# Output product of the mixture's rounds in two banks of its own and in three pieces, GpSimd's root ahead of its sums

## The reference, cut to what matters

```python
x = x + _L0_attn_ref(_layernorm(x), ...)            # ends with: out @ Wo + bo
x = x + _L0_xattn_ref(_layernorm(x), ctx_1024, ...) # out @ Wo + bo
x = x + _L0_ffn_ref(_layernorm(x), ...)
# in _L0_ffn_ref, up to the routing
rms = jnp.mean(xf * xf, axis=-1, keepdims=True)
normed = (xf * jax.lax.rsqrt(rms + EPS) * norm_weight).astype(jnp.bfloat16)
logits = (einsum('bsh,eh->bse', nf, gate_weight) + gate_bias)
scores, idx = jax.lax.top_k(logits, K)              # K = 2 of 8 experts
w = jax.nn.softmax(scores, axis=-1)
```

## Time and profile before

| what | us |
|---|---|
| runs: lowest, median, highest of 3 | 2040.12, 2045.48, 2047.65 |
| the profiled execution | 2038.56 |
| its span (first to last instruction) | 2036.8 |
| TensorE, VectorE, ScalarE, GpSimd busy in the span | 1861.0, 1299.9, 975.3, 970.7 |
| mean granted TensorE clock | 0.963 of full speed |

### The profile page before, as it was taken

How to read it: one execution, slowest core, us unless ns; L and a number is a source line. 1 busy time by engine, 2 the same in 40 slices (tenths; PEclk the granted TensorE clock), 3 DMA queues, 4 the chain that set the end, 5 groups by cost and what they waited for, 6 DMA issues and landing times.

```text
span 2036.8 us, 52538 instructions
## 1 busy us (share of the span) xinstructions
PE 1861.0 (91%) x21476; PEld 1544.5 (76%) x21476; DVE 1299.9 (64%) x2932; ACT 975.3 (48%) x1984; POOL 970.7 (48%) x783
## 2 busy tenths in 40 slices
PE   7999999999999999987649579999999999988994
PEld 5677777777777777766437479999899999987883
DVE  6667676767676766647756665456556554556983
ACT  3666666666666666532235233334443343344551
POOL 2555555555555555545633743344234333435441
PEclk9999999999999999999879789999999999999997
DMA  6101020101230100225134520000221000220000
GB/s 243 55 19 47 19 78 19 51 19 71 102 130 20 50 9 12 73 101 164 45 120 130 157 93 13 18 18 13 80 80 28 19 19 18 69 84 22 12 17 16
DMA packets 74606, 119.85 MB, mean 59 GB/s; under 512 B 8392, under 2 KB 64464, under 8 KB 70992
## 3 DMA queue, kind: packets, MB, share of 16 engines
q1 hardware_dynamic: 69392, 105.31, 15.4%
q0 software_dynamic: 2560, 6.30, 1.1%
q10 hardware_dynamic: 2416, 4.88, 0.7%
HBM read 76.61 MB, written 39.85 MB: 57 GB/s over the span
## 4 chain that ended last, share of the span: by engine, by line
PE 37%; POOL 5%; DVE 4%; DMA 3%; issue 3%; ACT 2%; SPq 1%; POOLq 0%; DVEq 0%; ACTq 0%
PE psum L265 12%; PE psum L276 8%; PE psum L2036 3%; PE psum L2024 2%; PE psum L2534 2%; PE psum L2010 1%; POOL b_yg L1487 1%; PE psum L225 1%; PE psum L2568 1%; POOL xs L1477 1%; PE psum L246 1%; PE psum L1352 1%; PE psum L1369 1%; ACT e_pr L2673 1%; DMA b_x_in<-in_x 1%
## 5 line engine op out<-in xcount | busy, mean ns | idle before, releaser
L774 POOL TENSOR_TENSOR a_sm<-a_sm,a_rsum 128x1024 f32<-128x1024 f32 x256 | 480.1, 1895 | 355.6 <-DVE a_rsum L808 353.2
L796 DVE CUSTOM_DVE_ANT_0 a_sm<-psum,a_strip 128x1024 f32<-128x1024 f32 x256 | 312.0, 1219 | 145.3 <-PE psum L628 145.3
L709 ACT ACTIVATE a_sm<-a_sm,a_mn 128x1024 f32<-128x1024 f32 x256 | 293.9, 1148 | 28.2 <-DVE a_mn L796 27.1
L714 ACT ACTIVATE a_pT<-psum 128x512 f32<-128x512 f32 x256 | 151.6, 592 | 272.4 <-PE psum L641 272.4
L641 PE MATMUL psum<-ident,a_sm 128*128 128x128 f32 x2048 | 275.2, 277 | 5.7 <-POOL a_sm L774 4.6
L641 PEld LDWEIGHTS psum<-ident,a_sm 128*128 128x128 f32 x2048 | 223.8, 140 | 62.9 <-issue 46.0
L656 PE MATMUL psum<-a_pT,a_V 128*64 128x256 f32 x2048 | 249.0, 385 | 0.6 <-ACT a_o L720 0.6
L656 PEld LDWEIGHTS psum<-a_pT,a_V 128*64 128x64 f32 x2048 | 136.1, 136 | 77.3 <-issue 22.1
L803 DVE COPY a_pT<-psum 128x512 f32<-128x512 f32 x256 | 174.9, 683 | 12.6 <-PE psum L641 5.4
L2120 ACT ACTIVATE g_val<-psum 128x512 f32<-128x512 f32 x64 | 38.0, 597 | 215.8 <-PE psum L2036 215.6
L628 PE MATMUL psum<-a_KH,a_QH 64*128 64x512 f32 x512 | 114.3, 443 | 2.5 <-DVE a_mn L796 2.5
(11 more groups left out here) (396 smaller groups left out, 3764.9 us busy)
## 6 DMA issues: line engine op xcount, KB each, us to landing
a_strip<-table SPq DMA_DIRECT2D x16, 960.0 KB, 6.7
oT<-a_o SPq DMA_DIRECT2D x64, 128.0 KB, 1.9
xs<-b_zeros SPq DMA_DIRECT2D x8, 1024.0 KB, 4.1
b_oT_in<-oT SPq DMA_DIRECT2D x7, 1024.0 KB, 5.7
y<-b_yb SPq DMA_DIRECT2D x23, 256.0 KB, 2.2
b_xs<-xs SPq DMA_DIRECT2D x23, 128.0 KB, 2.2
a_raw<-in_a_wqkv SPq DMA_DIRECT2D x7, 384.0 KB, 3.4
s_x<-in_x_rev SPq DMA_DIRECT2D x4, 512.0 KB, 8.2
```

The lines of the kernel that those rows point to most:

```text
L709: a.activation(sm[:, st % RING, :], sm[:, st % RING, :], ACT.Exp, scale=-1.0, bias=mn[:, at:at + 1], accum_out=rsum[:, at:at + 1]).then_in ...
L714: a.activation(probs(st, 0), psum[:, 4, :].rearrange("p (k q) -> p k q", k=4), ACT.Copy).then_inc(sig("pT_act"), 1)
L774: g.tensor_tensor(sm[:, st % RING, :], sm[:, st % RING, :], rsum[:, at:at + 1].broadcast_to([P, T]), ALU.mult).then_inc(sig("scaled"), 1)
L796: v.tensor_tensor_reduce(out=sm[:, st % RING, :], in0=scores_banks(hl).rearrange("p c n -> p (c n)"), in1=strip[:, pair % 2, hl, qt * P:qt ...
```

## The change

On TensorE the product `ay` gets two banks for itself and the other stages six. Its 16 steps are now three pieces: 2 steps (`ay_0`) behind `mT`, 6 (`ay_1`) behind `bs`, 8 (`ay_2`) behind `mr`. On GpSimd the root "mn" stands ahead of `first_sum`, and the sum of x1 last. The conversion of `w2` on ScalarE is made in two halves, in rounds 4 and 6, and whoever waited for two signals of `wide` waits for three.

```diff
-        every = [("ay", a + 1), ("mT", c), ("mg", c), ("bT", a), ("bp", b), ("by", b), ("bs", a), ("mr", c), ("ay_rest", a + 1)]
-        if r == 0:
-            every = [("ay", 1), ("ay_rest", 1)]
+        every = [("mT", c), ("ay_0", a + 1), ("mg", c), ("bT", a), ("bp", b), ("by", b), ("bs", a), ("ay_1", a + 1),
+                 ("mr", c), ("ay_2", a + 1)]
...
-            if stage != "ay_rest":
-                turns.add(sig, [(stage, s)], range(8))
+            if stage == "ay_0":
+                turns.add(sig, [("ay", s)], range(2))
+            elif stage[:2] != "ay":
+                turns.add(sig, [(stage, s)], range(2, 8))
...
-        sp.wait_ge(sig("wide"), 2)
+        sp.wait_ge(sig("wide"), 3)
...
-        def attended(s, t):
+        def attended(s, part):
             bank = banks("ay", s)
...
+            for i in range(*((0, 2), (2, HP), (HP, PT * HP))[part]):
+                t, k = i // HP, i % HP
...
+            if part == 2:
+                last.then_inc(sig("ay_ps"), 1)
...
-            if r == 4:
+            if r in (4, 6):
                 a.wait_ge(have("w2b"), 16)
-                a.activation(w2[:, :, :, :], w2b[:, :, :, :], ACT.Copy).then_inc(sig("wide"), 1)
+                some = slice(0, E0 // 2) if r == 4 else slice(E0 // 2, E0)
+                a.activation(w2[:, some, :, :], w2b[:, some, :, :], ACT.Copy).then_inc(sig("wide"), 1)
...
+            if b < NP:
+                norm_rstd(g, sig, "mn", b, mn, mhalf)
             if s + 1 < NP:
                 first_sum(s + 1)
-            if s < NP:
-                g.wait_ge(sig("bn_h"), PT * (s + 1))
-                g.tensor_tensor(x1[s % 2][:, :, :], x1[s % 2][:, :, :], over_tiles(bo_b[:, :], PT), ALU.add).then_inc(sig("x1_bo"), 1)
             if b < NP:
-                norm_rstd(g, sig, "mn", b, mn, mhalf)
                 g.wait_ge(sig("m_ss"), PT * (b + 1))
...
+            if s < NP:
+                g.wait_ge(sig("bn_h"), PT * (s + 1))
+                g.tensor_tensor(x1[s % 2][:, :, :], x1[s % 2][:, :, :], over_tiles(bo_b[:, :], PT), ALU.add).then_inc(sig("x1_bo"), 1)
```

More of the change, by code:

```diff
@@ L1258, in tensor @@
     def tensor(pe, then):
-        def attended(s, t):
+        def attended(s, part):
             bank = banks("ay", s)
[L1261 to L1264, removed]
+            for i in range(*((0, 2), (2, HP), (HP, PT * HP))[part]):
+                t, k = i // HP, i % HP
+                last = pe.matmul(bank[:, t * D:(t + 1) * D], (early["next"] if s == 1 else slots[s % 3])[0][:, k, t * P:(t + 1) * P],
+                                 wo[:, k, :], start=k == 0, stop=k == HP - 1)
+            if part == 2:
+                last.then_inc(sig("ay_ps"), 1)
         def attention(stage, s):
-            if stage == "ay":
+            if stage == "ay_0":
                 loaded(pe, s)
@@ L1270, in attention @@
                 banks.take(pe, "ay", s)
-                attended(s, 0)
-            elif stage == "ay_rest":
-                attended(s, 1).then_inc(sig("ay_ps"), 1)
+            if stage[:2] == "ay":
+                attended(s, int(stage[3]))
             elif stage == "bT":
@@ L1374, in tensor @@
         pe.wait_ge(have("w1"), 16 * (1 + E0))
-        pe.wait_ge(sig("wide"), 2)
+        pe.wait_ge(sig("wide"), 3)
         pe.wait_ge(sig("made"), 12)
```

## The result

The changed kernel takes 2052.02 us in the median of 7 runs (2049.26 to 2057.99), the kernel before, measured beside it, 2045.48 in the median of 7 (2040.12 to 2047.65). The ratio is 1.0048, with a 95% interval of 1.0030 to 1.0066: slower, by 6 to 13.5 us. I had forecast 0.7 us more and a change that cannot be measured, since I took about 10 us for what can be told from none; the interval leaves none out. The median lies within my range (2037 to 2053), close under its upper end.

What follows compares the result with a forecast made beforehand. It took the rounds to be bound by a ring of waits, closed by GpSimd and VectorE. Terms +1.8-3.1-1.8+1.2 = -1.9, plus 2.6 for the clock, gave +0.7 us on the median 2045.48: 2046 us, range 2037 to 2053.

Steps and rivals of the forecast that it cites:

- The order on TensorE: Rounds of the mixture: the bank wait goes, product steps move behind mT, bs and mr; 14.4 us from `joined` to `joined`.
- The order on GpSimd: Rounds of the mixture: root no longer behind the sums, squares slowed beside the first sum, ending at +11.65 us after `joined`.
- the ring of GpSimd and VectorE: The chain of waits between these engines from one `joined` to the next; 13.1 us, shorter than TensorE's 14.4.
- Rounds 2 to 6 without the clock: Five rounds at 14.4 us, 72.0 instead of 75.1 before: -3.1 us, leaving out falls of TensorE's clock.
- The clock, +2.6: Idle stretches before mT or h(1): three falls of TensorE's clock in seven rounds, 0.85 us each, together +2.6 us.
- the -1.8: Rounds 7 to 9: idle stretch before mT shortened, clock stays at 2.4 GHz, `crossed`(6) earlier; -1.8 us.
- Rival 2: TensorE's clock falls in every idle stretch before mT, seven times 1.69 us: +11.7, 2057 us; chance 0.06.
- Round 1: 14 instead of 8 product steps stand before `joined`(2), which comes at about 925.05: +1.8 us.
- Round 8: GpSimd's sum of x1 becomes free together with VectorE's `normed` and holds it by one sum: +1.2 us.
- ScalarE: Half conversions of w2 in rounds 4 and 6 are hidden, `pick`'s conversion by about 0.1 us; 0 in the sum.
- The 1.2 us that I had given it: `pick`'s conversion of 3.6 us on ScalarE would stand on the way with about 1.2 in a ring of 13.1.

Runs made afterwards that it cites:

- the filled wait: Changed kernel with five steps of the output product computed once more in the idle stretch before mT, results overwritten; ratio 0.9991 to the kernel before.
- five steps ahead: Changed kernel with the product in four pieces: 5 steps before mT, 2 behind it, 4 behind the scores, 5 behind the counts; ratio 0.9952 to the kernel before.
- first experiment: Kernel before with only GpSimd's new order (root ahead of the sums, sum of x1 behind the root of the squares); ratio 1.0007 to the kernel before.
- the filler elsewhere: Changed kernel with the same five repeated steps placed between the product's second and third piece, behind the scores; ratio 1.0080 to the kernel before.
- five steps ahead, GpSimd's old order: Changed kernel with five product steps before mT, but GpSimd's root and sum of x1 in their places of before; ratio 0.9977 to the kernel before.
- the two banks alone: Kernel before, order unchanged, with only the output product's two own banks, so its first half starts without waiting for `joined`; ratio 0.9981 to the kernel before.
- two steps in front of mT: Changed kernel with its first piece, two product steps, moved from behind mT to in front of it; ratio 1.0050 to the kernel before.

## Why the prediction was wrong, step by step

**The order on TensorE: right.** It gave 14.4 us a round at 2.4 GHz; with the wait filled it was 14.35. That `joined` would wait for TensorE in the changed kernel, and that GpSimd would no longer close the ring, was right too.

**The order on GpSimd: right.** The squares end 1.73 us behind the root (988.51 to 990.24) where 1.75 was forecast, and the ring of GpSimd and VectorE, 13.1 in the forecast, takes 13.3 in the run with five steps ahead.

**Rounds 2 to 6 without the clock, -3.1: right**, as the filled wait shows: 926.72 to 998.41 is 71.7 us, 72.0 forecast.

**The clock, +2.6: the step that failed.** Both factors of this term were too low. I took three falls in seven stretches, since the waits of 2.15 and 2.60 of the kernel before had none behind them. There was one in each of the seven. Those waits were followed at once by 3.5 us of product, and in the changed kernel the wait is followed by the thin stretch of transposes; but a wait of 2.42 us with the product behind it had one too (first experiment), so two waits without a fall could not tell how often it comes. What is shown of the cause is that filling the stretch ends the falls and the same work elsewhere does not; why one came every time stays open.

And I took 0.85 us for one, at most 1.69, as if the clock came back after 3.4 us as at 952.6, and as if waits would swallow part. It stayed down for 6.8, over bT, bp, by, bs and the first of the six steps, on the engine that closes the ring: 17.1-14.35 = 2.75 each. Even the kernel before had paid more than 1.69: its round with the fall took 17.64 us (951.49 to 969.13), 3.0 more than the next. Besides the half product's 1.69, a small addition of VectorE took 3.12 us (959.72 to 962.84) beside GpSimd's last scatter and its two sums, which ran until 962.81 (VectorE's timeline of the kernel before):

```profile
959.72 3.12 DVE L1617 TENSOR_TENSOR b_gap<-b_best 128x2 f32<-128x2 f32 x1
```

In the changed kernel, for rounds 2 to 6 that is 925.80 to 1011.36, 85.6 us, instead of 72.0: +13.6. In round 7 `crossed` comes 9.00 behind `joined`, at the lower clock, where I had 7.18: the -1.8 did not come. With the 1.4 us in round 1 beyond its forecast (below), the clock and what it set off cost 13.6+1.8+1.4 = 16.8 us, where my term was 2.6.

```profile
1020.36 0.69 DVE L1595 TENSOR_TENSOR b_x<-psum,b_x 128x512 f32<-128x512 f32 x1 [2.73 <-PE psum L1295]
```

Rival 2 had the mechanism, its place and every stretch; I gave it 0.06 and ended it at 2057, +11.7. Its price was too low (1.69 for 2.75), so it is in part luck that it ended between the two measures, +9.8 by the ratio and +14.6 in the profiled pair.

**Round 1: +1.8 forecast.** `joined`(2) came 13.92 behind `joined`(1) instead of 10.71 (923.24-912.53): +3.2, since by, bs and the first steps behind them met a fall (916.7 to 920.1): bs took 1.92 us for 1.13, the product's 14 steps 6.80.

**Round 8: right.** GpSimd's sum of x1 and VectorE's `normed` became free together, and VectorE took 1.87 for 0.88. Timelines of both engines, changed kernel:

```profile
1025.65 1.26 POOL L1530 TENSOR_TENSOR b_x1b<-b_x1b,b_bo_b 128x512 f32<-128x512 f32 x1
```

```profile
1025.71 1.87 DVE L1610 SCALAR_TENSOR_TENSOR b_nr<-b_xc,b_ss,b_nw 128x256 bf16<-128x256 bf16 x2 [0.19 <-POOL b_ss L1527]
```

That is +1.0 for the 1.2 forecast. The Trainium skill (SBUF — State Buffer, on SBUF's two separate sides) has VectorE's instructions with two SBUF inputs among those that need the port pair shared with GpSimd; this row, with both of its rows of values in SBUF and beside a sum of GpSimd that reads SBUF, agrees: 1.87 us for 0.88.

**ScalarE: right that it is hidden.** In round 5 the conversion of `pick` ended 1.05 us before nT:

```profile
975.41 3.60 ACT L1429 ACTIVATE b_pick<-b_seed 128x4096 bf16<-128x4096 f32 x1
980.06 0.60 ACT L1435 ACTIVATE b_nT<-psum 128x512 bf16<-128x512 bf16 x1 [1.05 <-PE psum L225]
```

Much of that room comes from the longer round. With the stretch filled, rounds of 14.35, the conversion ended at 972.52 and nT began at 972.65: hidden by about 0.1, as forecast. The 1.2 us that I had given it in a ring of 13.1 did not show: with five steps ahead round 5 took 13.32 us, round 6 13.25.

**The sum again, with measured terms**: round 1 +3.2, rounds 2 to 6 85.6-75.1 = +10.4, round 7 0, round 8 +1.0, together **+14.6** between the two profiled executions. The first expert's transposes start at 1054.37 instead of 1040.45, +13.9, and `joined`(1) had been 0.65 earlier. From there to the end of the span it is 1001.0 us against 996.4, in code that the change doesn't touch: 4.7 more, whose cause I have not followed. The medians differ by 6.5 us and the ratio says 0.48%, 9.8 us; the profiled pair differs by more (18.7 us between the executions), so its +14.6 is larger than what a usual pair would show.

## What to carry to other kernels

When work is moved out of a wait of TensorE, price what is left there: a stretch in which TensorE does little, wait and thin work together, can cost the clock of what stands behind it, here 2.75 us in each round for a saving of 0.2 (14.6 to 14.4). Sum an order twice, at both clocks, and keep enough real work in the stretch that recurs (five steps ahead gave 0.9952, two gave 1.0050). And a shorter way on one engine shows only once the other ring is out of its way: GpSimd's order was worth nothing alone and about 5 us, by intervals that just meet, with the better product order.

## What the runs showed of the hardware

- A fall of TensorE's clock lasted 6.8 us in each of the rounds 2 to 6 of the changed kernel, though TensorE was busy 6.3 of these 6.9 us (981.50 to 988.40); in the kernel before one lasted 3.4 under a full product. The work that runs at the lower clock can be dense in the records and still not bring it back at once. In the run with the filler elsewhere single falls lasted from 3.4 (952.2 to 955.6) to 10.2 us (969.3 to 979.5). Why they differ is not shown.
- Near-equal waits of TensorE did and did not have a fall behind them: 2.42 with and 2.58 without (GpSimd's order alone), 1.67 with (five steps ahead) and 2.77 without (five steps ahead, GpSimd's old order). No rule by the length of the wait comes out of these runs.
- A fall costs what the ring lets through: 2.75 us a round where TensorE closes the ring, 1.7 in the run with GpSimd's order alone, next to nothing with the two banks alone (14.64 to 14.96 us with a fall, 14.67 and 14.86 without).
- In the changed kernel the falls came once in each round: rounds of 17.06, 17.09, 17.11, 17.15 and 17.15 us, and of 15.9, 16.7, 16.9, 17.0 and 17.0 with two steps in front of mT, although there the wait was 0.9 us shorter. With the filler elsewhere the rounds varied between 17.4 and 20.1.
